# A mixture-of-experts kernel: the experts' rows are weighted, then scattered with an addition into a table of residual rows that is copied to the output

## What is computed

```python
def _L0_ffn_ref(x, gate_w, gate_b, W1, b1, W2, b2):
    probs = jax.nn.softmax(xf @ gate_w + gate_b, axis=-1)
    top2_vals, top2_idx = jax.lax.top_k(probs, 2)
    cw = jnp.zeros((N, Ee)).at[jnp.arange(N)[:, None], top2_idx].add(top2_vals)
    def step(acc, params):
        w1, bb1, w2, bb2, we = params
        h = jax.nn.gelu(xf @ w1 + bb1, approximate=False)
        y = h @ w2 + bb2
        return (acc + we[:, None] * y, None)
    ...
x = x + _L0_gnn_ref(...) + _L0_mix_ref(...)
x = x + _L0_ffn_ref(_layernorm(x)[None], ...)[0]
```

## Time and profile before

| what | value |
|---|---|
| median of 3 runs | 1417.63 us (1417.37 to 1419.28) |
| the profiled execution | 1413.7 us |
| its span, first to last instruction | 1411.7 us |
| the edge block | 199 to 939 us of the span |
| the combine block | 939 to 1101 us |
| the route block | 1101 to 1140 us |
| the experts block | 1140 to 1376 us |
| the finish block | 1376 to 1412 us |

### The profile page before, as it was taken

How to read it: one execution, slowest core, us unless ns; L and a number is a source line. 1 busy time by engine, 2 the same in 40 slices (tenths; PEclk the granted TensorE clock), 3 DMA queues, 4 the chain that set the end, 5 groups by cost and what they waited for, 6 DMA issues and landing times. The chain is left out here.

```text
span 1411.7 us, 26741 instructions
## 1 busy us (share of the span) xinstructions
PE 1120.5 (79%) x7285; PEld 865.7 (61%) x7286; DVE 968.9 (69%) x2208; ACT 824.8 (58%) x2932; POOL 739.4 (52%) x853
## 2 busy tenths in 40 slices
PE   6999746888888888888888888756676479999950
PEld 4777533666666666666666666536565269999950
DVE  7676238999999999999999999634663832112115
ACT  3444300777878787878777777852244047767730
POOL 4666267766666666666666666005321444555520
PEclk9999966899999999999999999989995689999985
DMA  8232458877777777777777777038001722222218
GB/s 230 96 119 95 107 152 253 235 225 210 217 210 213 214 209 216 207 214 209 216 208 216 211 216 213 18 119 274 19 19 56 233 75 70 67 67 67 70 38 272
DMA packets 132711, 225.07 MB, mean 159 GB/s; under 512 B 23555, under 2 KB 89098, under 8 KB 132594
## 3 DMA queue, kind: packets, MB, share of 16 engines
q0 software_dynamic: 43456, 138.49, 34.9%
q1 hardware_dynamic: 89138, 85.16, 20.0%
HBM read 191.18 MB, written 32.40 MB: 158 GB/s over the span
## 5 line engine op out<-in xcount | busy, mean ns | idle before, releaser
L568 POOL DMA_INDIRECT KV<-kv,ixs x464 | 456.9, 985 | 227.1 <-issue 115.1
L583 ACT ACTIVATE KV<-KV,WS 128x65 f32<-128x65 f32 x1856 | 469.7, 337 | 19.3 <-ACT RR L609 17.0
L669 PE MATMUL ps_o<-KV,PM 128*128 128x260 f32 x928 | 254.4, 397 | 18.7 <-DVE PM L764 8.5
L653 PE MATMUL ps_qe<-Q,PT 128*128 x1392 | 200.0, 283 | 3.9 <-DVE KV L753 3.9
L669 PEld LDWEIGHTS ps_o<-KV,PM 128*128 128x128 f32 x928 | 159.6, 192 | 64.8 <-issue 30.0
L653 PEld LDWEIGHTS ps_qe<-Q,PT 128*128 128x128 bf16 x1392 | 139.3, 101 | 53.8 <-issue 7.0
L675 PE MATMUL ps_o<-ACC,ident 128*128 x464 | 154.8, 416 | 0.0
L753 DVE TENSOR_TENSOR KV<-KV,ps_qe 128x512 f32<-128x512 f32 x232 | 147.6, 673 | 0.8 <-PE ps_qe L653 0.5
L759 DVE TENSOR_REDUCE S<-KV 128x16 f32<-128x1024 f32 x116 | 141.5, 1220 | 7.6 <-DVEq L815 0.5
L746 DVE TENSOR_TENSOR KV<-KV,ps_u 128x1024 f32<-128x1024 f32 x116 | 139.8, 1205 | 3.9 <-DMA KV<-kv,ixs 3.9
L1434 DVE TENSOR_TENSOR YG<-ps_y,B 128x256 f32<-128x256 f32 x56 | 23.8, 425 | 170.0 <-PE ps_y L1408 170.0
(11 more groups left out here) (299 smaller groups left out, 1670.8 us busy)
## 6 DMA issues: line engine op xcount, KB each, us to landing
dlb<-dl_rows SPq DMA_DIRECT2D x116, 128.0 KB
W<-in_f_W_dram SPq DMA_DIRECT2D x16, 512.0 KB, 6.0
tyb<-ty_rows SPq DMA_DIRECT2D x116, 64.0 KB
KV<-kv,ixs POOLq DMA_INDIRECT x464, 4.2
kv<-kvb SPq DMA_DIRECT2D x25, 258.0 KB, 2.6
xs_rows<-xs SPq DMA_DIRECT2D x25, 256.0 KB, 2.5
YF<-ytab SPq DMA_DIRECT2D x8, 640.0 KB, 9.2
VB<-kv SPq DMA_DIRECT2D x5, 650.0 KB, 9.0
```

The source lines that it names most:

```text
L568: pool.indirect_dma_start(kv[:, c % KR, n, :], None, d["kv"], bass.IndirectOffsetOnAxis(ap=T["ixs"][:, c % KR, n:n + 1], axis=0)).then_inc ...
L583: m = a.activation(part, part, ACT.Copy, scale=W[:, c % 2, s * H + h:s * H + h + 1])
L653: m = pe.matmul(T["ps_qe"][:, p % 3, k, :], T["PT"][:, h, (p % 2 * 2 + k) * P:(p % 2 * 2 + k + 1) * P], T["Q3"][:, bass.ds(at + n * C, C)] ...
L669: m = pe.matmul(T["ps_o"][:, p % 2, 0:A], PM[:, p % 2, k, :], kv[:, c % KR, 2 * x + k, C:KVW], start=(k == 0), stop=False)
```

## The change

The table `ytab` gives way to `acc`, one residual row for every node (3200) and one spare row for every slot. Four places change.

1. `phase_combine`: SP also stores `X` into `acc`, in five chunks of 640 KB, each ahead of the chunk of `xtab`.
2. `phase_route`: the product that finds the pairs of the slots also finds their gate values. `OHh` is now 128x112: POOL writes the left half times the pair's number (a second operation in its instruction), DVE the right half times the gate value, in an instruction of its own; `OHl` is the plain one-hot. The product is 112 wide, and a new tile `gate` holds each slot's gate value. The index arithmetic is reordered, since `DI` now names node rows.
3. `phase_experts`: DVE multiplies each tile of rows by its gate values after adding the bias. PE's output buffer is given back after the bias (`s_yb`), POOL's scatter waits for the product (`s_ye`). The scatter adds to the rows of `acc` in DRAM, and each scatter first waits until the one before it has landed, since a node's two rows can lie in two tiles.
4. `phase_finish` is gone. In the experts block SP waits for all scatters and copies `acc` to the output, DRAM to DRAM, 3120 rows and then 5 rows. The residual rows need no SBUF after the combine block.

```diff
@@ phase_combine, SP
             for c in range(NC_):
-
+                sp.wait_ge(s_res, c + 1)
+                sp.dma_start(d["acc"][c * CT_ * P:(c + 1) * CT_ * P, :].rearrange("(t p) c -> p t c", p=P), chunk(X, c)).then_inc(s_xt, 16)
                 sp.wait_ge(s_xf, (c + 1) * CT_)
                 sp.dma_start(d["xtab"][c * CT_ * P:(c + 1) * CT_ * P, :].rearrange("(t p) c -> p t c", p=P), chunk(Y, c)).then_inc(s_xt, 16)
@@ phase_route, POOL, DVE, PE
-                pool.tensor_scalar(T["OHh"][:, a % 4, :], T["iota_f"][:, 0:NB], T["hi_f"][:, a:a + 1], None, ALU.is_equal).then_inc(s_ohh, 1)
+                pool.tensor_scalar(T["OHh"][:, a % 4, 0:NB], T["iota_f"][:, 0:NB], T["hi_f"][:, a:a + 1], T["asg"][:, a:a + 1], ALU.is_equal,
+                                   ALU.mult).then_inc(s_ohh, 1)
...
-                v.tensor_scalar(T["OHl"][:, a % 4, :], T["iota_f"][:, :], T["lo_f"][:, a:a + 1], T["asg"][:, a:a + 1], ALU.is_equal,
+                v.tensor_scalar(T["OHh"][:, a % 4, NB:2 * NB], T["iota_f"][:, 0:NB], T["hi_f"][:, a:a + 1], gates[:, a:a + 1], ALU.is_equal,
                                 ALU.mult).then_inc(s_oh, 1)
+                v.tensor_scalar(T["OHl"][:, a % 4, :], T["iota_f"][:, :], T["lo_f"][:, a:a + 1], None, ALU.is_equal).then_inc(s_oh, 1)
...
             q(v.tensor_copy(vv, ps_inv[:, 128:128 + NB]))
-
+            q(v.tensor_copy(T["gate"][:, :], ps_inv[:, 128 + NB:128 + 2 * NB]))
...
-                pe.wait_ge(s_oh, a + 1)
+                pe.wait_ge(s_oh, 2 * a + 2)
                 pe.wait_ge(s_ohh, a + 1)
-                pe.matmul(ps_inv[0:NB, 0:P], T["OHh"][:, a % 4, :], T["OHl"][:, a % 4, :], start=(a == 0), stop=(a == NA - 1)).then_inc(s_mm, 1)
+                pe.matmul(ps_inv[0:2 * NB, 0:P], T["OHh"][:, a % 4, :], T["OHl"][:, a % 4, :], start=(a == 0), stop=(a == NA - 1)).then_inc(s_mm, 1)
@@ phase_experts, SP
+            for u in range(UE):
+                sp.wait_ge(s_sc[u], 16 * HB * NI)
+            whole = N // 16 * 16
+            sp.dma_start(d["out"][0:whole, :].rearrange("(a b) c -> a (b c)", b=13), d["acc"][0:whole, :].rearrange("(a b) c -> a (b c)", b=13)).then_inc(s_out, 16)
+            sp.dma_start(d["out"][whole:N, :], d["acc"][whole:N, :]).then_inc(s_out, 16)
+            sp.wait_ge(s_out, 32)
@@ phase_experts, POOL
                 pool.wait_ge(s_di, UE * j + u + 1)
-                pool.wait_ge(s_ye, (UE * j + u + 1) * HB)
+                pool.wait_ge(s_ye, UE * j + u + 1)
+                wait(pool, s_sc[(u - 1) % UE], (j + 1 if u else j) * 16)
                 pool.nop(nofuse=True)
-                for w in range(HB):
-                    pool.indirect_dma_start(d["ytab"], bass.IndirectOffsetOnAxis(ap=T["DX"][:, u, w:w + 1], axis=0),
-                                            YG[:, (u * HB + w) * C:(u * HB + w + 1) * C], None).then_inc(s_sc[u], 16)
+                pool.indirect_dma_start(d["acc"], bass.IndirectOffsetOnAxis(ap=T["DX"][:, u, 0:1], axis=0), YG[:, u * C:(u + 1) * C], None,
+                                        compute_op=ALU.add).then_inc(s_sc[u], 16)
@@ phase_experts, DVE
-                for w in range(HB):
-                    v.wait_ge(s_y, g * HB + w + 1)
-                    v.tensor_tensor(YG[:, (u * HB + w) * C:(u * HB + w + 1) * C], T["ps_y2"][:, (u % YB) * HB + w, 0:C], T["B2"][:, bass.ds(at, C)], ALU.add).then_inc(s_ye, 1)
+                rows = YG[:, u * C:(u + 1) * C]
+                v.wait_ge(s_y, g + 1)
+                v.tensor_tensor(rows, T["ps_y2"][:, u % YB, 0:C], T["B2"][:, bass.ds(at, C)], ALU.add).then_inc(s_yb, 1)
+                v.wait_ge(s_yb, g + 1)
+                v.tensor_tensor(rows, rows, T["gate"][:, bass.ds(g, 1)].broadcast_to([P, C]), ALU.mult).then_inc(s_ye, 1)
@@
-def phase_finish(nc, sem, T, d):
...
```

More of the change, by code:

```diff
@@ L1168, in phase_route @@
     ps_m, ps_inv = T["ps_m"], T["ps_inv"]
+    gates = T["PV"][:, :, :].rearrange("p r t -> p (r t)")
     with nc.Block() as block:
@@ L1252, in _ @@
             q(v.tensor_copy(vv, ps_inv[:, 128:128 + NB]))
+            q(v.tensor_copy(T["gate"][:, :], ps_inv[:, 128 + NB:128 + 2 * NB]))
+            q(v.tensor_scalar(t1, vv, float(NT * P), -float(NT * P), ALU.is_gt, ALU.mult))
+            q(v.tensor_tensor(vv, vv, t1, ALU.add))
+            q(v.tensor_scalar(T["slot"][:, :], T["slot"][:, :], float(NT * P + 1), None, ALU.add))
             q(v.tensor_scalar(t1, vv, 0.0, None, ALU.is_equal))
-            q(v.tensor_scalar(T["slot"][:, :], T["slot"][:, :], float(NA * P + 1), None, ALU.add))
             q(v.tensor_tensor(t1, t1, T["slot"][:, :], ALU.mult))
@@ L1259, in _ @@
             q(v.tensor_copy(T["DI"][:, :], t1))
-            q(v.tensor_scalar(t1, vv, float(NT * P), -float(NT * P), ALU.is_gt, ALU.mult))
-            q(v.tensor_tensor(vv, vv, t1, ALU.add))
             q(v.tensor_scalar(vv, vv, -1.0, 0.0, ALU.add, ALU.max))
@@ L1283, in phase_experts @@
     s_sc = [sem(f"ex_scattered{u}") for u in range(UE)]
-    s_gi, s_di, s_t, s_xt, s_wc, s_h, s_hg, s_y, s_ye = (sem("ex_" + n) for n in
-        ("gather_indices", "scatter_indices", "turned", "turned_copied", "weights_copied", "hidden", "activated", "rows", "rows_copied"))
+    s_gi, s_di, s_t, s_xt, s_wc, s_h, s_hg, s_y, s_yb, s_ye, s_out = (sem("ex_" + n) for n in
+        ("gather_indices", "scatter_indices", "turned", "turned_copied", "weights_copied", "hidden", "activated", "rows", "rows_biased", "rows_weighted",
+         "rows_out"))
     NI = NTILE // UE
@@ L1304, in phase_experts, with _ @@
     with nc.Block() as block:
+        @block.sync
+        def _(sp):
+            for u in range(UE):
[4 more added lines that the diff above has]
+            sp.wait_ge(s_out, 32)
         @block.gpsimd
@@ L1404, in tile @@
                 for w in range(HB):
-                    wait(pe, s_ye, (g - YB) * HB + w + 1)
+                    wait(pe, s_yb, (g - YB) * HB + w + 1)
                     for m in range(HC):
@@ L1437, in _ @@
             each_group_of_tiles(v, tile)
-def phase_finish(nc, sem, T, d):
[L1442 to L1470, removed]
-                            v.wait_ge(s_a, c * CT_ * 2 + t - c * CT_ + 1)
-                        n = LAST if t == NT - 1 else P
-                        v.scalar_tensor_tensor(out=X[0:n, t, :], in0=YF[0:n, r, t, :], scalar=T["PV"][0:n, r, t:t + 1], in1=X[0:n, t, :],
-                                               op0=ALU.mult, op1=ALU.add).then_inc(s_a, 1)
 DRAM_IN = ["x", "edges", "g_query", "g_Wq", "g_bq", "g_Wk", "g_bk", "g_Wv", "g_bv", "g_rel_w", "g_Wo", "g_bo", "g_gamma",
@@ L1489, in build @@
     d["xtab"] = nc.dram_tensor("xtab", (NT * P, C), F32).ap()
-    d["ytab"] = nc.dram_tensor("ytab", (2 * NT * P + NSLOT, C), F32).ap()
+    d["acc"] = nc.dram_tensor("acc", (NT * P + NSLOT, C), F32).ap()
     with ExitStack() as ctx:
@@ L1556, in build @@
             sbuf(ffn, {"W1": ((P, NEXP * W1C), F32), "W2": ((P, NEXP * HC * C), F32), "B2": ((P, NEXP * C), F32),
-                       "GI": ((P, NB), I32), "DI": ((P, NB), I32), "off": ((P, 3, NTILE), I32)})
+                       "GI": ((P, NB), I32), "DI": ((P, NB), I32), "gate": ((P, NB), F32), "off": ((P, 3, NTILE), I32)})
             with ExitStack() as ph:
@@ L1572, in build @@
                 phase_experts(nc, sem, T, d)
-        with ExitStack() as ph:
-            sbuf(ph, {"YF": ((P, 2, NT, C), F32)})
-            phase_finish(nc, sem, T, d)
 def lay_out(inputs):
```

11 lines of the change are left out of this document (5 added, 6 removed).

## The result

| | before | after |
|---|---|---|
| median (four runs each, us) | 1417.50 | 1444.51 |
| lowest and highest | 1414.1, 1419.28 | 1443.09, 1445.45 |
| the profiled execution | 1413.7 | 1444.96 |
| its span | 1411.7 | 1443.1 |

The changed kernel is 27.0 us slower, a ratio of 1.0193 with a 95% interval of 1.0171 to 1.0214. The prediction was 1436.5 us in a range of 1396 to 1480, with slower as the likeliest side.

The account below looks back on a forecast made before the run. No engine bounds the whole kernel; PE sets the experts block's 3.81 us a tile, then an uncovered tail. 7.0 + 0.2 + 0.45 + 38.0 - 26.8 = +18.9 us on 1417.6 gave 1436.5 us, range 1396 to 1480.

Parts of the forecast that it names:

- combine, five stores: Combine block: SP's five added 640 KB stores fit under some 17 us of cover by DVE, so no change.
- route: Route block: DVE's two one-hots lengthen 50 steps from 0.41 to 0.55 us, +7.0 us; the gate copy adds +0.2.
- DVE's product before the first scatter: Experts block: one more 128x256 product on DVE per tile delays the first scatter, +0.45 us.
- 55 steps: Experts block: each scatter waits for the last one's landing, so steps go from 3.81 to 4.5 us, +38.0 us.
- tail: Last scatter's issue to the end: 21.25 us with the DRAM copy against 48.0 before, -26.8 us.
- L = 3.7, the step 4.5: Experts block: an adding scatter takes 3.7 us from issue to landing; with POOL's 0.8 us wake, 4.5 us a step.
- a rival: Experts block: the addition is slow, for instance more POOL descriptor work; up to +105 us, 1523 us; step above 5.0, chance 0.18.
- the rival of the lost clock: Experts block: PE loses its clock through the gaps; would matter only at far longer steps; no chance of its own.
- The first rival: Experts block: the adding scatter lands within 3.0 us and the chain hides behind PE; -17.8 us, 1399.8 us; chance 0.23.
- The break-even of the prediction: Experts block: the sum of all terms is zero at a step of 4.16 us, a landing time of 3.36 us.
- the copy: Tail: copying 3.2 MB from DRAM to DRAM takes 13.7 us of data plus 2.8 fixed, 16.5 us.
- POOL's second operation hides as long as the instruction stays under that step: Route block: POOL's added operation, above its 0.438 us, costs nothing while its instruction stays under the 0.55 us step.

Follow-up runs that it names:

- Experiment 4: The changed kernel with POOL's one-hot back to one operation, the pair's number returned to DVE's one-hot: route block 42.5 us instead of 49.4, ratio 1.0112.
- Experiment 1: The changed kernel with the chain of waits kept but a plain scatter, no addition: ratio 0.988, 55 steps in 211.1 us.
- 3: The changed kernel with neither addition nor chain: plain scatters into a longer table, a row for every pair; ratio 0.9862, 55 steps in 209.6 us.
- 8: The kernel before, with the finish block's loads issued in the experts block once the scatters have landed: ratio 0.9973, tail 46.2 us.
- 9: The kernel before, with the whole finish block (loads, additions, stores) moved into the experts block, no barrier ahead: ratio 0.9913, tail 38.0 us.
- experiment 2: The changed kernel with adding scatters but no chain, into a longer table with a row for every pair: ratio 0.9854, 55 steps in 212.7 us.

## Why the prediction was right, and where it was off

| term, us | predicted | measured |
|---|---|---|
| combine, five stores | 0 | 0 to 1 (not clear of noise; taken as 0) |
| route | +7.2 | +10.7 |
| DVE's product before the first scatter | +0.45 | +0.5 |
| 55 steps | +38.0 | +46.5 |
| tail | -26.8 | -31.7 |
| sum | +18.9 | +26.0 |

The mechanism, the side and the order of the terms held. That the sum is only 7 us off is partly luck: the chain and the route block were taken 12.0 us too low, and the tail 4.9 us too dear. PE is idle for 0.6 us a tile behind its full clock, POOL waits on landings, and the kernel loses more in the chain than it wins in the tail. Without the chain or without the addition the same kernel is 21 to 26 us faster than before (18 to 22 by the stretches), which shows that this term decides the sign.

**The chain.** "L = 3.7, the step 4.5" came out as 3.8 and 4.66. Of the 8.5 us missed, 5.5 are the 0.1 in L; the rest is the wake, mostly a little over 0.8, and a few long steps (4.8 to 5.5 us for the first three, one of 5.3). But the parts of L were wrong although their sum was nearly right. A DRAM read ahead of the write (2.84 + 0.5) was taken and a doubled read of 0.35. The rows show a plain scatter of 2.4, plus 0.6 for POOL's work, which the prediction named only under a rival, plus 0.8 for data in packets of one row. That the two sums agree to 0.1 is luck. PE kept its full clock through the gaps (1.00 in the 50 us above), so the rival of the lost clock fell too.

The first rival, an addition that is hidden, fell with this. The Trainium skill, "Collectives: The Full Stack", Part 3, which counts only two source reads, would have L at 2.75 by the estimate of the prediction; the landing took 3.8, the data three times as long instead of twice, and POOL's 0.6 us is not in that rule. The break-even of the prediction, L = 3.36, stands between the two landings measured: the chain with 2.4 is hidden, with 3.8 it is not.

**The tail.** Right were SP's start and that the drain hides beside the copy. The mis-sized term is the copy: 16.5 us, taken from the middle between two rates plus 2.8 fixed, against 11.2. It moved at 342 to 399 GB/s, the rate of the finish block and so the lower bound of the time; that memory is both read and written did not bring it below that rate. The small second DMA cost 1.0 where 0.5 was taken, from no row. The Trainium skill, "DMA: Bandwidth & Descriptors" (Latency and other measured facts), has 207 to 214 GB/s for copies between DRAM tensors, of tiles with rows of 16 KiB at a wide pitch; for the flat copy here the measurement decides, and it is above. The error is some 5 us.

**The route block.** The step that failed is "POOL's second operation hides as long as the instruction stays under that step". It did not stay under: 0.61 against DVE's 0.475. The 0.55 for DVE was itself too high, which left the term only 3.5 us short; its lower bound had 0.17 for the 128x56 one-hot where the earlier trace rows have 0.192. The prediction had priced only the engine that got an instruction more, and not the one that got an operation more in an instruction that set the pace already. Experiment 4 shows it.

Two slips in the prediction's sums change nothing: 55 x 2.2 is 121 and not 123, and the low end of 1421 us leaves out the copy's bound, with which it is about 1416. The sum of the measured terms is 1.0 us under the difference of the medians, which is less than the untouched blocks vary by.

## What to carry to other kernels

When a change puts a completion wait between transfers that overlapped, the number to find is issue to landing plus wake, against the pace of the engine that bounds: here 3.2 us cost 1.5 us in 55 steps and 4.66 us cost 46. Look for which pairs of transfers can really meet, since waits at ten tiles, three of them in the first group, did the work of 55. And when a block ends in a barrier, see what each engine still has to do ahead of it (a drain, a row of issues): work placed in front of it, rather than behind it, gained 10 us with the same instructions, and half of that work in front gained nearly nothing.

## What the runs showed of the hardware

- An indirect scatter with an addition, of 128 rows of 1 KB: 1.59 us of POOL against 0.99, landing after 3.8 us against 2.4, 128 data packets against 32. All of this goes with the addition and stays when the chain is taken away.
- The chained step is that landing plus 0.76 to 0.86 us until POOL has started the next one. The same lag stands behind the plain scatter (0.83).
- A copy of 3.2 MB between DRAM tables, in 64 pieces of 50 KB, took 11.2 us.
- POOL's drain at the end of the experts block goes with the addition, and with nothing else that was changed. It took 9221 ns in all five profiles with a plain scatter (before, experiments 1, 3, 8 and 9) and 6276 ns in all seven with an adding one, with 112 indirect DMAs ahead of it each time. The cause is open. Experiment 1, without the addition, and experiment 2, without the chain:

```profile
L1309 POOLq DRAIN  x1: 9221/9221/9221, 1491.0 to 1491.0; - x1
```
```profile
L1310 POOLq DRAIN  x1: 6276/6276/6276, 1487.7 to 1487.7; - x1
```

- A second operation in POOL's 128x56 one-hot took its pace from 0.41 to 0.61 us, half as much again; beside a busier DVE the single operation had 0.475.
- In the changed route loop the granted clock stayed at its lower level, 1.2 GHz (0.50), though PE is shown busy for all of the 5 us; in the kernel before it had risen to 2.4 GHz (1.00) by 1123 us, with PE busy for 3.88 of 4. The two rows, after and before:

```profile
1136.00:1141.00 5.00, 5.00 (x18) 3.72 (x17) 4.05 (x17) 0.00 (x0) 5.00 (x9) 0.50 0.81 250
```
```profile
1123.00:1127.00 4.00, 3.88 (x21) 1.73 (x21) 3.43 (x11) 0.00 (x0) 4.00 (x11) 1.00 1.09 338
```

PE has 18 matmul records in 5 us, and 21 in 4 us before. The cause of the level is open. It is not what sets the pace of this loop: in experiment 4 the steps took 0.47 us while the clock was still at 0.50, and the same after it had risen.
